# Layer 0 cross attention: context probabilities computed keys first, with the maximum as a contraction row, in place of turned ones

## The reference

```python
q, k, v = split(x @ Wq), split(x @ Wk), split(x @ Wv)        # 32 heads of 16
q, k = rope(q), rope(k)
scores = einsum('bhqd,bhkd->bhqk', q, k) / 4 + attention_mask
w = softmax(maximum(scores, finfo.min))
out = einsum('bhqk,bhkd->bhqd', w, v)                        # 112 own keys
a_k, a_v = split(adapter @ Wk), split(adapter @ Wv)          # 375 context keys
a = tanh(gate) * softmax(einsum('bhqd,bhkd->bhqk', q, a_k) / 4)
out = out + einsum('bhqk,bhkd->bhqd', a, a_v)
return out @ Wo
```

## Time and profile before

| | us |
|---|---|
| median of 3 runs | 1869.06 |
| lowest and highest | 1868.19, 1871.84 |
| the profiled execution | 1871.72 |
| its span, first to last instruction | 1869.9 |
| PE busy in the span | 1792.0 (96%) |
| DVE busy | 998.8 (53%) |
| ACT busy | 606.0 (32%) |
| POOL busy | 409.6 (22%) |
| mean granted TensorE clock | 0.984 |

### The profile page before, as it was taken

One profiled execution on the slowest core, in us unless ns is written; L12 is line 12 of the kernel. 1 busy time (PEld: TensorE's weight loads), 2 busy tenths in 40 slices (PEclk: granted clock), 3 DMA queues, 4 the chain that ended last, 5 costly groups with the idle time before them and its releaser, 6 DMA issues.

```text
span 1869.9 us, 29060 instructions
## 1 busy us (share of the span) xinstructions
PE 1792.0 (96%) x11730; PEld 1179.7 (63%) x11730; DVE 998.8 (53%) x1892; ACT 606.0 (32%) x1931; POOL 409.6 (22%) x488
## 2 busy tenths in 40 slices
PE   7999999999999999999889999998999999999998
PEld 6766666646665665666555888876577674444444
DVE  4765666426666666557644111116645455565887
ACT  1233222315555565555640111110312213232511
POOL 2432323512020220120003000006121020002476
PEclk9999999999999999999998999999999999999999
DMA  9100002000000000000214988965000021643011
GB/s 377 42 1 1 1 1 107 1 15 18 18 18 15 4 18 18 1 17 2 113 69 174 368 331 327 339 254 198 27 1 1 1 107 50 250 161 124 3 38 40
DMA packets 31109, 170.62 MB, mean 91 GB/s; under 512 B 3865, under 2 KB 3865, under 8 KB 17185
## 3 DMA queue, kind: packets, MB, share of 16 engines
q1 hardware_dynamic: 28416, 161.43, 22.9%
q0 software_dynamic: 2560, 7.34, 1.3%
HBM read 155.91 MB, written 16.52 MB: 92 GB/s over the span
## 4 chain that ended last, share of the span: by engine, by line
PE 83%; DVE 9%; POOL 4%; ACT 2%; issue 2%; DMA 1%; SPq 0%; POOLq 0%; DVEq 0%
PE PS L1142 8%; PE PS L985 6%; PE PS L1222 6%; PE PS L936 6%; PE PS L1019 5%; PE PS L1058 4%; PE PS L1010 4%; PE PS L1286 4%; PE PS L1182 4%; PE PS L1151 4%; PE PS L1255 3%; PE PS L1042 3%; PE PS L1273 3%; PE PS L1078 2%; PE PS L993 2%
## 5 line engine op out<-in xcount | busy, mean ns | idle before, releaser
L2046 POOL TENSOR_TENSOR rstd<-veps,mhalf 112x1 f32<-112x1 f32 (+1 forms) x76 | 58.0, 764 | 577.2 <-DVE veps L1315 554.0
L1142 PEld LDWEIGHTS PS<-R,W 128*128 128x128 f32 x1344 | 155.8, 195 | 11.8 <-issue 11.8
L1142 PE MATMUL PS<-R,W 128*128 128x128 f32 x1344 | 156.2, 278 | 2.2 <-DVE R L1610 2.2
L1439 DVE TENSOR_REDUCE nmx<-PS 112x2 f32<-112x750 f32 x128 | 114.0, 931 | 81.4 <-PE PS L1042 81.4
L1910 ACT ACTIVATE R<-PS,nmx 112x375 f32<-112x375 f32 x256 | 142.9, 573 | 3.7 <-DVE nmx L1439 3.7
L936 PE MATMUL PS<-xT,W 128*128 128x224 f32 x640 | 127.1, 359 | 1.1 <-DMA W<-in_w0kv 0.8
L936 PEld LDWEIGHTS PS<-xT,W 128*128 128x128 f32 x640 | 123.0, 194 | 7.7 <-issue 5.5
L1617 DVE TENSOR_TENSOR R<-R,PS 128x512 f32<-128x512 f32 x21 | 14.5, 688 | 201.7 <-PE PS L1142 201.7
L1387 DVE TENSOR_TENSOR x<-x,PS 112x512 f32<-112x512 f32 x40 | 27.5, 687 | 170.0 <-PE PS L985 82.4
L1255 PE MATMUL PS<-W 128*128 128x512 f32 x256 | 117.6, 602 | 0.0
L985 PE MATMUL PS<-W,R 128*112 128x512 f32 x256 | 113.7, 597 | 0.0
(11 more groups left out here) (291 smaller groups left out, 3233.7 us busy)
## 6 DMA issues: line engine op xcount, KB each, us to landing
W<-in_we SPq DMA_DIRECT2D x63, 1024.0 KB, 8.3
W<-in_entwT SPq DMA_DIRECT2D x8, 1024.0 KB, 7.3
W<-in_entpw SPq DMA_DIRECT2D x8, 1024.0 KB, 8.5
W<-in_ctxT SPq DMA_DIRECT2D x8, 750.0 KB, 4.2
R<-in_ctxT SPq DMA_DIRECT2D x8, 750.0 KB, 8.4
R<-in_ctx SPq DMA_DIRECT2D x8, 750.0 KB
xs_rows<-in_x SPq DMA_DIRECT2D x3, 1792.0 KB, 38.2
R<-xs_rows SPq DMA_DIRECT2D x21, 256.0 KB, 9.1
```

The lines of the kernel that those rows point to most:

```text
L1142: o = e.matmul(PS[:, m, c * 128:(c + 1) * 128], gate_up(j % 3, k, off + c * 128), BT[:, j % 2, k, :], start=k == 0, stop=k == 3)
L1439: e.tensor_reduce(nmx[0:S, par, r:r + 2], PS[0:S, r:r + 2, 0:SC], AX.X, ALU.max, negate=True).then_inc(*up("cmax", (b, c, par, r)))
```

## The change

The probabilities of the context are no longer turned. The context scores are computed twice: first as before, with queries on partitions, for the maximum; then with keys on partitions and queries along the columns, so that their exponentials are already laid out as the values' product reads them. A maximum per query can't be a bias in that layout, where queries are columns. So it is brought in as a row of the contraction:

- The queries of one head use 16 of the 32 rows of a row group; the other 16 are zero. VectorE writes the negative maxima into `NM`, in the column that belongs to a free row of each row group; `xq` turns `NM` on TensorE and `qa` adds it to `QM`. The context's keys are now kept twice (`KcT[..][par]`), with a one in that row and zeros in the other head's rows (`ones_at`, `parity`). `xst` then gives scores minus maximum, and `ce` is a single exponential of 125 x 4 x 336.
- The sums come with the values: a column of ones in the free columns of `VX` and `Vc` (`one_at`) makes the sum of the probabilities one of the 32 rows of the result. `xd`, now once for each column of a batch, spreads it over the partitions with a shuffle and takes the reciprocal of the whole 128 x 448 tile on VectorE; POOL multiplies it with `gain` (one, or the tanh of the gate) and with the values and adds the four parts. `xr`, `xb` and VectorE's sums go.
- There are two tasks for each column, one for each `par`, and each holds own and context scores, in one bank side by side. `slot` writes the order: `xst` needs the maximum of its own slot, the values follow two slots later, and the mixed-in steps come in three windows with the shares 0.3, 0.25 and 0.45. `ck`, `cv`, `vx` and `xw` are cut in halves so that they fit them.
- The scratch for descriptors of POOL's transfers is 4096 bytes, and the gate comes as four columns.

```diff
+TASKS = [(b, c, par) for b in range(NBATCH) for c in range(4) for par in range(2)]
+SHARE = (0.3, 0.25, 0.45)
+def slot(n, fill):
+    out = []
+    here, behind, last = [TASKS[m] if 0 <= m < len(TASKS) else None for m in (n, n - 1, n - 2)]
+    if here:
+        out += [("xc", *here), ("cm", *here, 0), ("cm", *here, 2)]
+    if last:
+        out += [("xv", *last), ("xcv", *last), ("xu", *last)]
+        if last[2]:
+            out.append(("xd", *last[:2]))
+    out += fill[0]
+    if behind:
+        out.append(("xt", *behind))
+    if here:
+        out += [("xq", *here), ("xm", *here, 0), ("qa", *here)]
+    out += fill[1]
+    if here:
+        out += [("xst", *here), ("ce", *here), ("xm", *here, 1), ("xm", *here, 2), ("xe", *here)]
+    return out + fill[2]
...
+            def xq(b, c, par):
+                m = bank(("xq", b, c, par))
+                w.wait_ge(*at("cmax", (b, c, par, 2)))
+                t = e.transpose(PS[:, m, 0:S], NM[0:S, par, :], ident[0:S, 0:S])
+                t.then_inc(*up("p_turned", ("xq", b, c, par)))
+            def xst(b, c, par):
+                z, i = (b // UB) % 2, b % UB
+                w.wait_ge(*at("masked", (b, c, par)))
+                w.wait_ge(*at("qa", (b, c, par)))
+                for t_ in range(3):
+                    for r in range(4):
+                        ro = slice(32 * r, 32 * r + 32)
+                        o = e.matmul(PS[0:KC, r, bcol(t_)], KcT[b % 2][par][ro, c, t_ * KC:(t_ + 1) * KC],
+                                     QM[z][ro, c, par, bcol(i)], start=True, stop=True)
+                o.then_inc(*up("scores", ("xst", b, c, par)))
-            def xct(b, c, par, t_):
-                m = bank(("xct", b, c, par, t_))
-                for r in range(4):
-                    w.wait_ge(*at("cexp", (b, c, par, r)))
-                    t = e.transpose(PS[0:KC, m, bcol(r)], p_of(b, c, par)[0:S, r, t_ * KC:(t_ + 1) * KC], ident[0:S, 0:S])
-                t.then_inc(*up("p_turned", ("xct", b, c, par, t_)))
...
+            def qa(b, c, par):
+                q = QM[(b // UB) % 2][:, c, par, bcol(b % UB)]
+                w.wait_ge(*at("p_turned", ("xq", b, c, par)))
+                e.tensor_tensor(q, q, PS[:, bank_of["xq", b, c, par][0], 0:S], ALU.add).then_inc(*up("qa", (b, c, par)))
+            def xd(b, c):
+                z = c % 2
+                w.wait_ge(*at("ou", (b, c, 1)))
+                if b or c >= 2:
+                    w.wait_ge(*at("oxt", (b, c - 2) if c >= 2 else (b - 1, c + 2)))
+                for par in range(2):
+                    e.stream_shuffle(SH[:, z, par], OU[:, z, par], [(16, 0)[par]] * 32).then_inc(*own())
+                settled()
+                e.reciprocal(SH[:, z], SH[:, z]).then_inc(*up("recip", (b, c)))
...
+            def ce(b, c, par):
+                w.wait_ge(*at("scores", ("xst", b, c, par)))
+                e.activation(PC[0:KC, par], PS[0:KC, 0:4, 0:3 * S], ACT.Exp).then_inc(*up("cexp", (b, c, par)))
...
+            def xd(b, c):
+                w.wait_ge(*at("recip", (b, c)))
+                w.wait_ge(*at("gain", 1))
+                t = SH[:, z].rearrange("p a k n -> p (a k) n")
+                e.tensor_tensor(t, t, gain[:, c].rearrange("p a k -> p (a k)").unsqueeze(2).to_broadcast([128, 4, S]),
+                                ALU.mult).then_inc(*up("g_own", ("xd", b, c, 0)))
+                sem = done(0)
+                e.tensor_tensor(SH[:, z], SH[:, z], OU[:, z], ALU.mult).then_inc(*sem)
+                sem = done(1)
+                e.tensor_tensor(SH[:, z, 0], SH[:, z, 0], SH[:, z, 1], ALU.add).then_inc(*sem)
+                w.wait_ge(*at("g_own", ("xd", b, c, 2)))
+                e.tensor_tensor(OXT[:, b % 2, c, :], SH[:, z, 0, 0], SH[:, z, 0, 1], ALU.add).then_inc(*up("oxt", (b, c)))
```

More of the change, by code:

```diff
@@ L228, in projectx @@
     return out + [("rt", *behind)]
+HALF = ("ck", "cv", "vx", "xw")
 def context(b):
[L232 to L282, removed]
@@ L293, in cross @@
 def cross():
-    out, gaps = [], attendx()
+    out = []
     for b in range(NBATCH):
-        fill = context(b + 1) + [("load", "ct", b + 2)] * (b + 2 < NBATCH) + [("vx", b + 1)] if b + 1 < NBATCH else [("load", "front", j) for j in (1, 2, 0)]
+        fill = context(b + 1) + [("load", "ct", b + 2)] * (b + 2 < NBATCH) + values_x(b + 1) if b + 1 < NBATCH else [("load", "front", j) for j in (1, 2, 0)]
         if b % UB == 0 and b // UB + 1 < NU:
@@ L306, in cross @@
         late = expert_rows(range(6)) if b == NBATCH - 1 else []
[L307 to L312, removed]
-                fill += late
[L314 to L322, removed]
-    h = part(range(5))
[L324 to L328, removed]
+        fixed = {(3, 2): [("xw", b - 1, 0)], (4, 0): [("xw", b - 1, 1), ("stats", 2, b - 1)]} if b else {}
+        unit = sum(cost(s) for s in fill + late) + sum(cost(s) for some in fixed.values() for s in some)
+        unit, due = unit / 8, 0.0
+        for i in range(8):
+            if i == 2:
+                fill += late
+            windows = []
+            for k in range(3):
+                some = fixed.get((i, k), [])
+                due += unit * SHARE[k] - sum(cost(s) for s in some)
+                while fill and (due > cost(fill[0]) / 2 or (i, k) == (7, 2)):
+                    due -= cost(fill[0])
+                    some.append(fill.pop(0))
+                windows.append(some)
+            out += slot(8 * b + i, windows)
+    h = part(range(5))
+    out += slot(len(TASKS), [h[:1], h[1:2], []]) + slot(len(TASKS) + 1, [h[2:5], [], []])
+    return out + [("xw", NBATCH - 1, 0), h[5], ("xw", NBATCH - 1, 1), ("stats", 2, NBATCH - 1)]
 def experts():
@@ L546, in psum_use @@
         return anyx, 1, [("pj", a)]
+    if k in HALF and a[-1]:
+        return (), 0, []
     if k == "vx":
[L548 to L552, removed]
-    if k == "xc":
[L554 to L560, removed]
+        return anyx, 1, [("vx", a[:1])]
+    if k == "ck":
+        return anyx, 1, [(("even_out", "odd_out")[a[1] % 2], step[:3])]
+    if k == "cv":
+        return anyx, 1, [(("even_out", "odd_out")[a[1] % 2], step[:3])]
+    if k == "xc":
+        return (0, 1, 2, 3), 4, [[("cexp", a), ("masked", a)]] * 4
+    if k == "xt":
+        return LOW, 1, [("even_out", step)]
+    if k == "xq":
+        return LOW, 1, [("qa", a)]
     if k == "xw":
-        return LOW, 1, [("x", step)]
+        return LOW, 1, [("x", step[:2])]
     if k == "route":
@@ L607, in place @@
     bank, past = {}, {}
-    taken, frees = [-1] * 8, [None] * 8
-    late = False
+    taken, frees = [-1] * 8, [[] for _ in range(8)]
+    late, held = False, set()
     for n, step in enumerate(order):
@@ L995, in pj, with half, vx @@
                 o.then_inc(*up("proj", ("pj", u, c, which)))
-            def vx(b):
-                m = bank(("vx", b))
+            def half(step):
+                first = (*step[:-1], 0)
+                return bank_of[first][0] if step[-1] else bank(first)
+            def vx(b, h):
+                m = half(("vx", b, h))
                 w.wait_ge(*at("xT", (1, b)))
                 w.wait_ge(*at("d_q2", "wx"))
-                for k in range(4):
+                for k in (2 * h, 2 * h + 1):
@@ L1106, in route, with xw @@
+            def xw(b, h):
+                m = half(("xw", b, h))
+                w.wait_ge(*at("d_q3", "wx"))
+                w.wait_ge(*at("oxt", (b, 3)))
+                for c in (2 * h, 2 * h + 1):
+                    o = e.matmul(PS[0:S, m, :], OXT[:, b % 2, c, :], Wx[3][:, c, :], start=c == 0, stop=c == 3)
+                if h:
+                    o.then_inc(*up("attended", ("xw", b)))
             def route():
@@ L1893, in cv, with vx, ck @@
-            def cv(b, t):
-                if t % 2 == 0:
+            def vx(b, h):
+                if h:
+                    w.wait_ge(*at("proj", ("vx", b)))
+                    w.wait_ge(*at("zeros", f"x{b % 2}"))
+                    e.activation(pairs(VX[b % 2][0:S, :]), by_pair(PS[0:S, bank_of["vx", b, 0][0], :]), ACT.Copy).then_inc(
+                        *up("vx", (b,)))
+            def ck(b, c, h):
+                if h and c % 2 == 0:
+                    w.wait_ge(*at("context", ("ck", b, c)))
+                    for par in range(2):
+                        o = e.activation(KcT[b % 2][par][:, c, :], PS[:, bank_of["ck", b, c, 0][0], 0:SC], ACT.Identity,
+                                         bias=C("ones_at")[:, par:par + 1], scale=C("parity")[:, par:par + 1])
+                    o.then_inc(*up("even_out", ("ck", b, c)))
```

348 lines of the change are left out of this document (147 added, 201 removed), and 3 rows, old and new, of the table COST.

## The result

The changed kernel takes 2029.0 us (median of four runs, 2024.9 to 2035.1) against 1868.6 for the kernel before: a ratio of 1.086, 95% interval [1.083, 1.089]. The profiled execution has a span of 2022.8 us, 152.9 more than before; it is the fastest of its four, and so lies 4 us under their median. The cross attention now runs from 432.2 to 1125.5 us: 693.3 us against 547.0. Everything behind it takes 897.3 us, as before (897.2), so neither the smaller descriptor scratch nor anything else there costs time; 6.5 us are lost ahead of it, where the context's keys and values of the first batch are made.

What follows compares the result with a forecast made beforehand. TensorE's own work was taken to bound the cross attention's first seven batches. 1869.9 + 83 (seven batches) + 15 (last batch) + 15 (clock) = 1983, or 1982 as runs measure; chance 0.62, own range 1935 to 2020, 8 in 10 1905 to 2030.

Steps and rivals of the forecast that it cites:

- clock as second cost: Rival: each of some 40 TensorE waits is followed by a spell at the lower clock; 2020 to 2040 us, chance 0.15.
- signs of being wrong: Reciprocal under 1 us, waits before xc instead, or TensorE's busy time in the cross attention not falling.
- TensorE's work: Cross attention, per batch: 12.5 us removed, 9.4 added, net 3.1 less; 25 over eight batches if nothing waited.
- The reciprocal: In xd on VectorE, every second slot, ahead of qa: 448 elements take 2.85 us, 32 times, 91 us in all.
- Waits in the seven batches: TensorE waits 15 us a batch, mostly at xst in slots with xd; less 3.1 of work, +83 us over seven.
- The last batch: Eighth batch, with little to fill its slots: chains of 70 us and a tail of 20, 90 against 75.4, +15.
- The clock: Cross attention at 0.93: about 440 us of work lose 31, half taken as lying in waits; +15, bounds 0 and +50.
- A short reciprocal: Rival: 448 elements at a tensor operation's pace, xd 1.4 us instead of 3.75; still slower, 1914 us, chance 0.15.
- Ahead of the stage: Before the cross attention: nothing moves before 425 us but by the shift.

Runs made afterwards that it cites:

- run 1: The changed kernel with xd's reciprocal of 448 columns replaced by a copy of eight columns and the normalisation left out; 1911.5 us.
- run 2: The changed kernel with xd moved to the end of its slot, behind the own scores' subtraction, instead of ahead of the query correction; 1918.8 us, ratio 1.0255.
- Run 3: The changed kernel with the reciprocal taken three times in place instead of once; 2246.6 us.
- Run 4: The changed kernel with three unused products of 512 columns on TensorE ahead of the wait at xst in each slot with xd; 2016.4 us, ratio 1.0767.
- the first run of experiment 5: The kernel before with an unused reciprocal of 112x448 behind each of the 32 own sums on VectorE, ahead of the mask addition; 1938.4 us, ratio 1.0369.

## Why the prediction was right, and where its size was off

The forecast was slower by 113 us, to 1982; measured were 160. The direction was right, and so was the mechanism: the reciprocal ahead of `qa` makes TensorE stand at `xst`. The size was not. 2029.0 lies outside the prediction's own range for this case (1935 to 2020) and only 1 us inside its wider one (1905 to 2030); it lies in the band of the rival "clock as second cost" (2020 to 2040), which was given 0.15 against 0.62 for the forecast. One of the prediction's signs of being wrong also came true: TensorE's busy time in the stage did not fall. That sign was badly chosen, since busy time holds both the work, which fell, and the clock, which more than undid it. By its steps:

- **TensorE's work.** I took 25 us off. To take the clock out of the measured busy time, I overlapped the matmul records with the spells of the lower level and halved what lay in them. By this estimate the stage is at full clock 486.9 us of work against 514.4, 27.5 less. It is borne out by runs 1, 2 and 3, which have the same TensorE instructions at clocks from 0.80 to 0.95: it gives 488.7, 489.6 and 484.6.
- **The reciprocal.** 2.85 us from the straight line through three small sizes; measured 2953 ns in all 32:

```profile
L1429 DVE RECIPROCAL R<-R x32: 2952/2953/2954, 463.5 to 1113.7; 128x448 f32<-128x448 f32 x32
```

Run 3 shows that it lay on the path with all its length, run 1 that it and what followed from it are 117 of the 160 us. The Trainium skill, "VectorE: DVE Perf Modes", section "First, the fixed hardware budget", states a repeat count of 8; with the 0.96 GHz of "Trainium Kernel Development and Optimization" that gave an estimate of 3.7 us. The measurement does not agree with this estimate.
- **Waits in the seven batches.** I took 15 us a batch, 105. Idle time of TensorE rose there from 10.4 to 108.7 us, so by 98. The sum was right, its parts less so: 72 us of it are waits at the correction, and 15 came where I had not looked, at the bank of a mixed-in product behind VectorE's copies. With the clock's share the batches took 78 to 90 us, four of the seven longer than the 76 to 85 that I gave.
- **The last batch.** +15 predicted, +27 measured (102.8 against 75.4): 19 of waits, 15 of clock, 7 less work. My +15 held no clock, so it stands against 12.
- **The clock.** This is the term that was mis-sized. I took +15, with +50 as its bound. By the same overlap the lower level cost TensorE 66 us of the stage after, and 9 before: +56. The failed step is "At 0.93 about 440 us of work lose 31, of which I take half as lying in waits". The stage ran at 0.89, the last batch at 0.73, and hardly any of the loss was hidden: of 150 us at the lower level TensorE was at work for 131.5. Its 27 spells each begin in a wait of TensorE or within 1.5 us of its end, and last over the mixed-in products that follow, as the half `ck` of 2.87 us shows. The rival "clock as second cost" named this and had the right size, though its own terms don't give its band: 68 us on top of 1967 is 2035, but half of that, as it says, is 2001. Run 4 confirms the cause from the other side: with the waits filled the clock is at 0.95, and by the same overlap the lower level costs 31 us in place of 66. It shows in the kernel before too: in the first run of experiment 5, TensorE's idle time rises by 36 us and the cost of the lower level by 31 (from 9 to 41), so nearly half of its 70 us is clock.
- **A short reciprocal.** The rival's 1914 us is what run 1 measured (1911.5), though not by its terms: the rival put 5 us to the clock, and run 1 lost 15 to it by the overlap.
- **Ahead of the stage.** I expected no change before 425 us; 6.5 us came. From 364 us on TensorE is idle for 8.1 us where it was for 3.7: once 6.6 us for POOL instead of 3.7, and 1.3 for ScalarE's copies of a `ck` into the doubled keys. Its busy time there is 60.1 us against 58.0, at a clock of 0.92 against 0.94. No run tries what causes this.

The account of the stage, seven batches and the last: 98 + 19 waits, 41 + 15 clock, less 21 + 7 of work: +145 of the 146.3 (rounded terms).

## What to carry to other kernels

On an in-order engine ask what stands ahead of the instruction that the bound engine waits for, and not how busy the engine is: the same 32 instructions were worth 8, 70 or 117 us by their place, and moving one step cured 110 of 160 us. The work mixed in as cover has waits of its own, for its PSUM bank above all; if these hang on the engine that is late, it covers nothing. And where waits of a few microseconds come back in every loop, price the clock too: here it was a third of the loss. Last, the step that costs most is not all: without any reciprocal the new order was still 43 us behind the old one.

## What the runs showed of the hardware

A reciprocal on VectorE costs by its columns: 164, 203 and 541 ns for 1, 8 and 64 and 2953 ns for 448, about 6.2 ns a column, almost five times a tensor operation of that size (0.61 us); it is cheap on sums before they are spread and dear behind. One exponential of 125x1344 on ScalarE takes 1291 ns, where four of 112x375 with their sums took 0.57 and 0.21 each in the kernel before. Four `float32` records on the four row groups of 32 partitions run side by side: in the `xst` at 773.80 they start within 0.02 us, and such rounds follow each other at 0.11 us. Its 24 records took 0.92 us including their fill and drain, three fifths of the 1.56 us that turning the same probabilities took the earlier trace rows.
